# x's layer norm ahead of the slot search, and another split of the table copies, in the setup of a graph network kernel

## What is computed

```python
h = jnp.maximum(_layernorm(x, axis=-1), 0.0)
x = x + _L0_gnn_ref(h, L0_gnn_weight, src, dst, edge_type_16)

# _L0_gnn_ref, weight (16, 64, 64):
h_src = feat[src]
for r in range(num_rels):
    mask = etypes == r
    msg = msg + h_src * mask[:, None].astype(feat.dtype) @ weight[r]
out = jax.ops.segment_sum(msg, dst, num_segments=feat.shape[0])
```

## Time and profile before

| what | value |
|---|---|
| median of 3 runs | 2432.45 us (2432.16 to 2432.92) |
| profiled execution | 2440.53 us, its span 2438.6 us |
| busy: PE, DVE, ACT, POOL | 1427.3, 741.7, 191.1, 1610.6 us |
| chain that ended last, by engine | POOL 54%, issue 22%, PE 16%, DVE 5%, DMA 2%, ACT 1% |
| first gather of the first layer starts | 77.12 us |

### The profile page before, as it was taken

One profiled execution on the slowest core, in us unless ns is written; L12 is line 12 of the kernel. 1 busy time (PEld: TensorE's weight loads), 2 busy tenths in 40 slices (PEclk: granted clock), 3 DMA queues, 4 the chain that ended last, 5 costly groups with the idle time before them and its releaser, 6 DMA issues.

```text
span 2438.6 us, 36361 instructions
## 1 busy us (share of the span) xinstructions
PE 1427.3 (59%) x7642; PEld 1254.6 (51%) x7643; DVE 741.7 (30%) x2432; ACT 191.1 (8%) x311; POOL 1610.6 (66%) x1693
## 2 busy tenths in 40 slices
PE   5586666666433333333577657666574336767686
PEld 2386666666433333333466546555443236656575
DVE  5311111111511111111532222222442234444456
ACT  3000000000000000000211111111220000000000
POOL 2577777776577777776377777777127777777530
PEclk9655555555555555555655565565655555555555
DMA  6621111111111111111233333332063323222210
GB/s 195 219 43 27 26 26 26 26 26 23 32 26 26 26 26 26 26 26 24 49 72 68 66 65 65 65 65 54 6 256 83 78 75 78 79 77 77 57 42 14
DMA packets 159011, 144.41 MB, mean 59 GB/s; under 512 B 109905, under 2 KB 111855, under 8 KB 158802
## 3 DMA queue, kind: packets, MB, share of 16 engines
q0 software_dynamic: 53888, 69.64, 13.9%
q1 hardware_dynamic: 105058, 73.94, 10.4%
HBM read 113.55 MB, written 37.28 MB: 62 GB/s over the span
## 4 chain that ended last, share of the span: by engine, by line
POOL 54%; issue 22%; PE 16%; DVE 5%; DMA 2%; ACT 1%; SPq 0%; DVEq 0%; POOLq 0%; ACTq 0%
POOL flat L467 49%; PE ps L1200 8%; POOL uvT L467 5%; PE ps L1190 5%; PE ps L1042 1%; DMA table<-flat 1%; PE ps L1016 1%; PE ps L1025 1%; DVE var L545 0%; PE ps L1055 0%; DVE uvT L538 0%; DMA flat<-table,flat 0%; DVE mean L536 0%; DVE ps L870 0%; DVE h L560 0%
## 5 line engine op out<-in xcount | busy, mean ns | idle before, releaser
L467 POOL DMA_INDIRECT flat<-table,flat x1248 | 1194.3, 957 | 491.0 <-issue 379.7
L1055 PE MATMUL ps<-flat,oh 128*128 128x64 f32 x1664 | 469.2, 431 | 490.7 <-DMA flat<-table,flat 482.4
L1055 PEld LDWEIGHTS ps<-flat,oh 128*128 128x128 f32 x1664 | 406.5, 331 | 503.9 <-issue 503.9
L627 DVE TENSOR_SCALAR oh<-iota_n,drel 128x128 f32<-128x128 f32 x1248 | 264.0, 299 | 1052.2 <-PE ps L1055 631.9
L467 POOL DMA_INDIRECT uvT<-table,idx x416 | 399.5, 960 | 230.3 <-issue 125.6
L1190 PE MATMUL ps<-qn,oh_bytes 128*128 x1248 | 164.8, 235 | 188.6 <-issue 111.0
L1190 PEld LDWEIGHTS ps<-qn,oh_bytes 128*128 128x128 bf16 x1248 | 128.7, 104 | 227.0 <-issue 198.6
L1057 PEld LDWEIGHTS ps<-ones,oh 128*128 128x128 f32 x832 | 227.3, 333 | 0.0
L1057 PE MATMUL ps<-ones,oh 128*128 128x1 f32 x832 | 221.3, 335 | 0.0
L1200 PE MATMUL ps<-flat,oh 128*128 128x65 f32 (+1 forms) x832 | 188.1, 420 | 9.9 <-DVE oh L814 5.2
L1200 PEld LDWEIGHTS ps<-flat,oh 128*128 128x128 f32 x832 | 180.6, 331 | 15.5 <-issue 13.7
(11 more groups left out here) (259 smaller groups left out, 873.6 us busy)
## 6 DMA issues: line engine op xcount, KB each, us to landing
table<-flat SPq DMA_DIRECT2D x52, 512.0 KB, 3.6
oh_bytes<-slot_node SPq DMA_DIRECT2D x104, 256.0 KB, 3.4
flat<-table,flat POOLq DMA_INDIRECT x1248
flat<-edge_attr_padded SPq DMA_DIRECT2D x416, 16.0 KB
uvT<-table,idx POOLq DMA_INDIRECT x416
edge_attr_padded<-edge_attr SPq DMA_DIRECT2D x1, 6250.0 KB
xs<-x SPq DMA_DIRECT2D x1, 768.0 KB
flat<-L_gnn_weight SPq DMA_DIRECT2D x2, 256.0 KB, 3.9
```

The costliest lines, as they stand in the source:

```text
L467: nc.gpsimd.indirect_dma_start(dest[:, b, j, :], None, table, at_).then_inc(gat[b], 16)
L627: last = V.tensor_scalar(oh[:, b, j, :], iota_n[:], drel[:, bass.ds(g * SG + j, 1)], None, ALU.is_equal)
L1055: last = T.matmul(acc[:, bass.ds(n[j] * D, D)], oh[:, b, j, :], rows_[:, j, :], start=False, stop=True, skip_group_check=True)
```

## The change

The norm of x moves ahead of most of the slot search, x's small piece is loaded before `dst`, and the first halves of the table tiles are shared out anew: VectorE copies those of tiles 0 to 5 and of 18 to 25, ScalarE those of 6 to 17. The constants are EARLY = 6 and AHEAD = 18. The spread of `reach` goes to another part of `aux`, and its turning of `slot_n` into a row goes behind tile 5 on TensorE.

```diff
-        INIT, INIT_W = 6, 4
+        INIT, INIT_W = 5, 4
-        AHEAD = 14
+        EARLY, AHEAD = 6, 18
...
             sp.dma_start(xs[:, 0:TN - 1, :], a["x"][0:(TN - 1) * P, :].rearrange("(t p) d -> p t d", p=P)).then_inc(s("x_in"), 16)
+            sp.wait_ge(s("xs_clear"), 1)
+            sp.dma_start(xs[0:NLAST, TN - 1, :], a["x"][(TN - 1) * P:N, :]).then_inc(s("x_in"), 16)
             sp.dma_start(dst_rows[:, 0:SC - 1, :], a["dst"][0:(SC - 1) * P * P].rearrange("(c p k) -> p c k", p=P, k=P)).then_inc(s("dst_in"), 16)
...
-            sp.dma_start(xs[0:NLAST, TN - 1, :], a["x"][(TN - 1) * P:N, :]).then_inc(s("x_in"), 16)
...
+            V.memset(xs[:, TN - 1:NT, :], 0.0).then_inc(s("xs_clear"), 1)
             V.memset(fill_i[:], -1).then_inc(s("init"), 1)
...
+            def table_half(n):
+                dve.wait_ge(s("tab_ps"), n + 1)
+                stage_free(dve, 0, n)
+                V.tensor_copy(stage[:, n % 4, 0:512], acc[:, (n % 2) * 1024:(n % 2) * 1024 + 512]).then_inc(s("tabA"), 1)
...
             dve.wait_ge(s("x_in"), 32)
-            for t0, t1 in HALVES:
-                centred(xs, t0, t1)
+            centred(xs, *HALVES[0])
+            dve.wait_ge(s("dst_in"), 32)
+            dve.wait_ge(s("const"), 9)
...
+            V.tensor_tensor(reach[:], reach[:], slot_t[:], ALU.add).then_inc(s("reach"), 1)
+            centred(xs, *HALVES[1])
             rectified()
+            link(V.memset(pack[:, SC - 1, :, :], 0))
+            dve.sem_inc(s("pack_clear"), 1)
+            dve.wait_ge(s("reach_row"), 1)
+            for c in range(SC):
...
+            V.tensor_scalar(slot_n128[:], slot_n[:], float(P), None, ALU.mult).then_inc(s("slot_t"), 1)
+
+            for n in range(EARLY):
+                table_half(n)
+            dve.wait_ge(s("rows_ps"), 1)
+            n_ps = aux[0:1, 512:512 + SLOTS].rearrange("o (g j) -> o g j", j=SG)
+            link(V.tensor_copy(n_slots, n_ps))
...
+            dve.wait_ge(s("tabA"), AHEAD)
             for n in range(AHEAD, NT):
-                dve.wait_ge(s("tab_ps"), n + 1)
-                stage_free(dve, 0, n)
-                V.tensor_copy(stage[:, n % 4, 0:512], acc[:, (n % 2) * 1024:(n % 2) * 1024 + 512]).then_inc(s("tabA"), 1)
+                table_half(n)
...
-                if n < AHEAD:
+                if n == EARLY:
+                    act.wait_ge(s("tabA"), EARLY)
+                if EARLY <= n < AHEAD:
                     A.copy(stage[:, n % 4, 0:512], acc[:, at_:at_ + 512]).then_inc(s("tabA"), 1)
...
-            for n in range(AHEAD - 2):
+            for n in range(EARLY):
                 table_ps(0, n)
+            pe.wait_ge(s("slot_t"), 1)
+            for c in range(SC):
+                last = T.transpose(aux[0:1, 512 + START[c]:512 + START[c] + P], slot_n[:, c:c + 1], ident[:])
+            last.then_inc(s("rows_ps"), 1)
+            for n in range(EARLY, AHEAD - 2):
+                table_ps(0, n)
```

More of the change, by code:

```diff
@@ L508, in _, with stage_free @@
             V.memset(dst_rows[:, SC - 1, :], 0).then_inc(s("init"), 1)
-            V.memset(xs[:, TN - 1:NT, :], 0.0).then_inc(s("init"), 1)
             V.memset(dprev[:, SC - 1, :], 0).then_inc(s("init"), 1)
             V.memset(dnext[:, SC - 1, :], 0).then_inc(s("init"), 1)
[L513 to L527, removed]
-            dve.wait_ge(s("rows_ps"), 1)
-            n_ps = aux[0:1, 512:512 + SLOTS].rearrange("o (g j) -> o g j", j=SG)
-            link(V.tensor_copy(n_slots, n_ps))
+            def stage_free(eng, l, n):
+                before = l * len(range(n % 4, NT, 4)) + n // 4
+                if before:
+                    eng.wait_ge(tab[n % 4], 16 * before)
+            def table_half(n):
+                dve.wait_ge(s("tab_ps"), n + 1)
+                stage_free(dve, 0, n)
+                V.tensor_copy(stage[:, n % 4, 0:512], acc[:, (n % 2) * 1024:(n % 2) * 1024 + 512]).then_inc(s("tabA"), 1)
             sums, squares = [0], [0]
@@ L562, in _ @@
             dve.wait_ge(s("x_in"), 32)
-            for t0, t1 in HALVES:
-                centred(xs, t0, t1)
-            rectified()
+            centred(xs, *HALVES[0])
+            dve.wait_ge(s("dst_in"), 32)
+            dve.wait_ge(s("const"), 9)
+            link(V.tensor_scalar(reach_i[:], dst_rows[:, :, P - 1], 7, None, ALU.arith_shift_right))
+            link(V.tensor_tensor(reach[:], reach_i[:], iota_tile[:], ALU.add))
+            link(V.tensor_scalar(slot_t[:], iota_tile[:], float(TE - 1), 1e6, ALU.is_ge, ALU.mult))
+            V.tensor_tensor(reach[:], reach[:], slot_t[:], ALU.add).then_inc(s("reach"), 1)
+            centred(xs, *HALVES[1])
+            rectified()
+            link(V.memset(pack[:, SC - 1, :, :], 0))
+            dve.sem_inc(s("pack_clear"), 1)
+            dve.wait_ge(s("reach_row"), 1)
+            for c in range(SC):
+                link(V.tensor_scalar(work[0][:, :, :].rearrange("p c k -> p (c k)"), aux[:, 1024:1024 + SC * P], iota_slot[:, c:c + 1], None, ALU.is_lt, ALU.add, accum_out=slot_t[:, c:c + 1]))
+            link(V.tensor_copy(slot_ti[:], slot_t[:]))
+            link(V.tensor_tensor(slot_n[:], iota_slot[:], slot_t[:], ALU.subtract))
+            V.tensor_scalar(slot_n128[:], slot_n[:], float(P), None, ALU.mult).then_inc(s("slot_t"), 1)
[4 more added lines that the diff above has]
+            link(V.tensor_copy(n_slots, n_ps))
             link(V.tensor_copy(n_words, n_slots[:, :, 0]))
@@ L1001, in _ @@
             for c in range(SC):
-                last = T.matmul(aux[:, c * P:(c + 1) * P], reach[:, c:c + 1].broadcast_to([P, P]), ident[:], start=True, stop=True)
+                last = T.matmul(aux[:, 1024 + c * P:1024 + (c + 1) * P], reach[:, c:c + 1].broadcast_to([P, P]), ident[:], start=True, stop=True)
             last.then_inc(s("reach_row"), 1)
-            pe.wait_ge(s("slot_t"), 1)
-            for c in range(SC):
-                last = T.transpose(aux[0:1, 512 + START[c]:512 + START[c] + P], slot_n[:, c:c + 1], ident[:])
-            last.then_inc(s("rows_ps"), 1)
             def node_transposes(src, *ready):
```

4 lines of the change are left out of this document (removed).

## The result

The changed kernel takes 2425.09 us (median of 10 runs, 2423.06 to 2427.89), the kernel before 2432.70 us (median of 10 runs, 2431.11 to 2437.68). The ratio is 0.997 with a 95% interval of 0.9961 to 0.9978, so the change saves 7.6 us, by the interval 5.4 to 9.5 us. The forecast was 2424.4 us, 8.05 us less than before. The profiled execution took 2425.92 us with a span of 2424.1 us.

What follows compares the result with a forecast made beforehand. GpSimd's gathers bound the kernel, their start at 77.12 us set by VectorE's order and the emptying of table pairs. 8.18 + 0.96 - 0.2 - 0.89 = 8.05 us, from 2432.45 to 2424.4 us; range 2422.5 to 2427.7.

Steps and rivals of the forecast that it cites:

- transposes of h earlier: On TensorE in the setup: with x's norm first, h's transposes start at 16.25 in place of 24.43, 8.18 us earlier.
- two low-clock pairs shorter: First two tile pairs on TensorE at 1.2 GHz: VectorE's copying beside ScalarE saves 0.48 us on each.
- slot row, ScalarE alone: Table pairs from the third on: slot transposes cost 0.2 us, ScalarE alone for tiles 6 to 17 costs 0.89 us.
- last product to first gather: Setup's end: 4.62 us passed here before the change, and the sum counted no gain or loss.
- x: Load of x, loaded first: VectorE's mean was taken to start at 6.7 us, between 6.0 and 7.5.
- The rival that it rises one pair earlier: TensorE's clock is up by the second pair: 1.6 us more, a gain of 9.6, 2422.8 us; chance 0.10.
- Slot row: Four slot transposes behind tile 5 on TensorE, about 0.5 us: the third pair becomes 3.4 us in place of 3.21.
- The moved gathers: GpSimd's twelve pack gathers, 7.1 us later: kept at 16.5 us, with bounds of 15.0 and 24.8.
- cover of 1.7 us: VectorE at tile 18: casts end at 53.5, its table half is wanted at 55.2, the thinnest cover of the change.
- signs of being right: Expected in the trace: mean of x at 6.0 to 7.5, slot_t near 21, casts before tile 18, first gather near 69.
- rival 3: Index chain ends last; each microsecond beyond 1.7 passes on: gain 4.7 (2427.7) or 1.4 us (2431.0); chance 0.09.
- Rival 5: The change does nothing: the gain is eaten between 77.12 us and the program's end, 2432.4 us; chance 0.02.

Runs made afterwards that it cites:

- the fifth experiment: The changed kernel without any edit, run beside the kernel before on another chip; median 3036.17 us, ratio 1.0005 (0.9983 to 1.0028).
- the six buffers: The changed kernel with six staging buffers for table tiles in place of four, on another chip; median 3036.01 us, ratio 1.001 (0.9991 to 1.0029).
- the last experiment: The changed kernel with its twelve pack gathers held back until twelve table tiles are copied; one run, 3027.84 us, the kernel before 3014.86 beside it.
- a quarter of the bytes: The changed kernel writing only 256 of 1024 columns of tiles 0 to 11 in place, the rest zero-filled at the end; one run, 3055.38 us.
- the early clock: The changed kernel with 26 unread identity products on TensorE ahead of the first products, to raise its clock; median 3002.91 us, ratio 0.9977 (0.9956 to 0.9997).

## Why the prediction was right

The mechanism was right: h comes earlier because VectorE no longer does the search first, and the table keeps up. The sum is close term by term, by the rows above against the earlier trace rows:

| term | predicted | measured |
|---|---|---|
| transposes of h earlier | 8.18 | 24.43 - 15.81 = 8.62 |
| two low-clock pairs shorter | 0.96 | (38.11 - 28.24) - (28.69 - 19.62) = 0.80 |
| slot row, ScalarE alone (third pair to the last product's end) | -1.09 | (72.50 - 38.11) - (64.04 - 28.69) = -0.96 |
| last product to first gather | 0 | 4.62 - 4.96 = -0.34 |
| sum | 8.05 | 8.12 |

The terms miss by 0.44, -0.16, 0.13 and -0.34 us. That the sum is within 0.07 of the forecast is luck in part.

- **x.** 6.54 for the mean, within 6.0 to 7.5 and 0.16 before the value taken. The insert between the halves cost 0.68 us (9.14 to 9.82) and not 0.83: its four operations start 0.20 us apart in both kernels, but the next one starts 0.08 us after the last and not 0.22. Another 0.13 came from the rest of the norm.
- **Low-clock pairs.** 4.57 and 4.50 us from start to start, forecast 4.56 and 4.35. The clock rose at the third pair, as forecast. The rival that it rises one pair earlier happened too, with the same kernel in the fifth experiment (24.26, 2.58 us); in the unaltered run beside the six buffers it rose at the third pair. So it is not a matter of the kernel.
- **Slot row.** The third pair takes 3.03 us with it, not 3.4. The product records beside it need 2.58 us, less than the 2.86 that had been taken, because VectorE's help is still there for tiles 4 and 5 (its copies at 30.71 start with ScalarE's) and the pair never waits. The third line of the table hides this: the third pair came out 0.37 us better, and from the fourth pair to the last product's end it took 32.32 us (31.72 to 64.04) where the working has 29.14 + 2.93 = 32.07. The late half of tile 18 is among what was lost there.
- **The moved gathers.** The quick end of the bounds was right: 14.7 us and not 16.5. VectorE was idle or reading PSUM for most of that time.
The Trainium skill (SBUF — State Buffer, section "Who interferes with whom") says that a VectorE instruction with at most one SBUF input, outside the two-port modes, doesn't contend with GpSimd; the spacing of 1.25 us beside the table halves agrees.
- **The cover of 1.7 us is the term that was mis-sized.** The working moved `slot_t` and everything behind it by 7.1 us, and so took over from before the 1.46 us between the last gather's issue (31.48) and the index work (32.94). After, that stretch is 36.62 to 41.42, 4.80 us, 3.3 more. It ate the 2.0 us by which the last issue came earlier than the working has it (36.62 and not 38.58) and 1.4 more. With casts that end 1.4 us late (54.88 and not 53.5) and a table that asks 0.4 us early (54.80 and not 55.2), nothing was left of 1.7. So one of the signs of being right, that VectorE's casts end before tile 18 is ready, did not come. What had been named in rival 3, "table writes now share the DMA engines with the pack gathers", is what happened. The gathers' issue was quick and their landing slow, and it cost about 0.3 us because the cover hid the rest. The DMA issues with their median time to landing show it, before in 28 to 33 us, after in 30 to 42 us:

```profile
flat<-dst_shifted,slot_ti POOLq DMA_INDIRECT x2, 2.3
```

```profile
table<-flat SPq DMA_DIRECT2D x7, 512.0 KB, 4.8
flat<-dst_shifted,slot_ti POOLq DMA_INDIRECT x4, 5.3
```

The gathers of the changed kernel land after 5.3 us, and the table's writes beside them after 4.8 us, where they took 2.8 before (40 to 56 us). From 30 to 41 us the share of the DMA engines is 1.01 and 1.02:

```profile
30.00:36.60 6.60, 5.67 (x23) 2.56 (x21) 5.32 (x17) 3.23 (x6) 5.07 (x6) 1.00 1.01 359
36.60:41.40 4.80, 4.48 (x14) 1.61 (x11) 1.12 (x4) 3.26 (x7) 0.02 (x1) 1.00 1.02 410
```

That the traffic is the reason rests on the table of the last experiment, where the step falls with the share and goes back to 1.42 us at 0.08.

- **Rival 5, that the lead is lost later**, is excluded for the first chip by the medians: 7.6 us (5.4 to 9.5) against 8.12 at the first gather. On the other chips the fifth experiment shows no gain at the end.
- **What stays open.** On the other chips two runs of the changed kernel have their first gather at 74.64 and 77.60 us, a lead of 2.5 us and none against 77.12. There the forecast of the setup would have been wrong, by a stall that the result's profiled execution doesn't show. The last experiment points to the pack gathers in flight beside the writes, which alone don't bring it about; two more buffers and a quarter of the bytes don't remove it. ScalarE waits there for TensorE's signal on a tile, which comes up to 7.15 us behind the start of its products, where 2.00 is usual. Why it comes late was not found. Whether the early clock pays on the first chip could not be tried there; here its gain of about 4 us at the fourth pair was lost in that stall.

## What to carry to other kernels

Moving a step later moves its DMAs into other traffic, so their time to landing must be costed anew from a stretch with that traffic, not carried along from the old place. Two changes that are worth little alone can be worth much together: the norm first needs the later AHEAD, since what becomes late must not be wanted early. Where a cover is a microsecond or two, look at who released the instruction behind it even when the total came out right.

## What the runs showed of the hardware

- The same program takes a quarter longer on other chips: 2432.70 against 3007 to 3034 us for the kernel before. In the profiles of the unaltered changed kernel (spans 2424.1 and 3037.8 us) a gather instruction takes about the same (952 and 959 ns); the idle time ahead of the 1248 gathers goes from 477.5 to 866.9 us and that ahead of the last layer's 416 from 230.2 to 440.8, together 600 of the 614 us. What makes the difference between the chips is not shown.
- An indirect gather beside full DMA engines lands late: 5.3 us (median) at a DMA share of 1.01 to 1.02, 2.3 us before the table's writes begin, for the same twelve gathers.
- In nine of the eleven profiles with indirect gathers in flight beside the table's writes, and in none of the three where they stand apart, TensorE stopped for 2.2 to 6.1 us ahead of one of its first eight pairs, and ScalarE with it. Where the trace has the event, ScalarE's wait ended with TensorE's semaphore, up to 7.15 us after the start of the pair's products where 2.00 is usual at the full clock.
- Behind pauses of 3.3 to 6.1 us TensorE's granted clock was 0.50, and where a pair has a row of its own its products took 4.4 to 4.7 us in place of 2.93.
